# Sixteen instead of eighteen embedding fields by one-hot lookup in a recommender tower, 23 instead of 21 by gather

## What is computed

```
e = stack([tbl_f[ids[:, f]] for f in 0..38], axis=1)      # 2048 x 39 x 64
z = sum over e of (inner_w @ e)**2                        # 2048 x 128
h = concat([z, dense_ctx], axis=1)                        # 2048 x 144
h = relu(h @ W_top1 + b_top1); h = relu(h @ W_top2 + b_top2)
y = h @ W_top3                                            # 2048 x 1
```

## Time and profile before

| | us |
|---|---|
| median of 3 runs (704.07 to 708.3) | 704.64 |
| the profiled execution, whole time | 704.59 |
| its span, first to last instruction | 702.8 |
| mean granted TensorE clock in it | 0.84 of full |

### The profile page before, as it was taken

One profiled execution on the slowest core, in us unless ns is written; L12 is line 12 of the kernel. 1 busy time (PEld: TensorE's weight loads), 2 busy tenths in 40 slices (PEclk: granted clock), 3 DMA queues, 4 the chain that ended last, 5 costly groups with the idle time before them and its releaser, 6 DMA issues.

```text
span 702.8 us, 10016 instructions
## 1 busy us (share of the span) xinstructions
PE 485.0 (69%) x3376; PEld 413.2 (59%) x3376; DVE 442.3 (63%) x708; ACT 226.9 (32%) x310; POOL 353.6 (50%) x343
## 2 busy tenths in 40 slices
PE   0466322767666877779685977777879677987556
PEld 0356322656655756677574856675767666875334
DVE  0988022759686647767676847774778558945542
ACT  2333000323322333334322433324323243445542
POOL 6888775655656554565645545746465365000000
PEclk9987656989898896989988988999798899996756
DMA  8416113667556636655555746754576445645660
GB/s 226 105 51 175 26 25 81 147 146 181 136 131 156 154 83 148 155 128 147 148 135 117 183 102 142 168 139 111 139 166 147 115 123 134 150 107 147 150 165 0
DMA packets 59024, 91.17 MB, mean 130 GB/s; under 512 B 14155, under 2 KB 21064, under 8 KB 58962
## 3 DMA queue, kind: packets, MB, share of 16 engines
q1 hardware_dynamic: 35244, 57.07, 33.1%
q10 hardware_dynamic: 12984, 22.47, 11.6%
q0 software_dynamic: 10752, 11.03, 8.5%
HBM read 27.19 MB, written 0.08 MB: 39 GB/s over the span
## 4 chain that ended last, share of the span: by engine, by line
PE 37%; issue 18%; DVE 16%; DMA 11%; another core or an unknown queue 9%; SPq 4%; ACT 3%; ACTq 1%; DVEq 0%
PE side L400 17%; DMA xs<-xl 8%; DVE onehot L606 6%; PE delta L452 5%; PE turned L441 5%; DVE zp L626 4%; PE side L423 4%; PE side L416 3%; DVE x_all L620 2%; SPq L264 2%; DVE xl L614 2%; ACT sq_all L517 1%; PE side L428 1%; DMA idh<-ids 1%
## 5 line engine op out<-in xcount | busy, mean ns | idle before, releaser
L358 POOL DMA_INDIRECT x_all<-tbl,idx x336 | 352.9, 1050 | 243.8 <-issue 124.9
L400 PE MATMUL side<-table,onehot 125*128 125x192 bf16 x2496 | 275.7, 273 | 119.0 <-issue 69.4
L400 PEld LDWEIGHTS side<-table,onehot 125*128 125x128 bf16 x2496 | 235.2, 109 | 158.5 <-issue 115.6
L517 ACT ACTIVATE sq_all<-delta 128x1024 f32<-128x1024 f32 x128 | 130.8, 1023 | 119.8 <-PE delta L452 54.3
L452 PE MATMUL delta<-xs,ws 117*128 117x512 f32 x240 | 120.8, 532 | 69.3 <-issue 29.0
L626 DVE TENSOR_REDUCE zp<-sq_all 128x128 f32<-128x2048 f32 x64 | 146.1, 2282 | 19.9 <-ACT sq_all L517 15.1
L620 DVE TENSOR_REDUCE x_all<-side 128x128 f32<-128x384 f32 x144 | 78.7, 552 | 114.3 <-remote 72.5
L606 DVE TENSOR_SCALAR onehot<-idh,row_no 125x1024 bf16<-125x1024 f16 (+1 forms) x352 | 137.5, 458 | 17.6 <-DMA idh<-ids 17.6
L503 ACT ACTIVATE xh<-turned 117x512 fp32r<-117x512 f32 x96 | 53.8, 561 | 232.4 <-PE turned L441 93.2
L614 DVE TENSOR_TENSOR xl<-turned,xh 117x512 fp32r<-117x512 f32 x96 | 61.6, 642 | 71.8 <-ACT xh L503 42.7
L452 PEld LDWEIGHTS delta<-xs,ws 117*128 117x128 f32 x240 | 50.7, 224 | 82.7 <-issue 40.2
(11 more groups left out here) (32 smaller groups left out, 93.1 us busy)
## 6 DMA issues: line engine op xcount, KB each, us to landing
xs<-xh ACTq DMA_DIRECT2D x80, 234.0 KB
xs<-xh SPq DMA_DIRECT2D x80, 234.0 KB
xs<-xl SPq DMA_DIRECT2D x80, 234.0 KB
x_all<-tbl,idx POOLq DMA_INDIRECT x336
idh<-ids SPq DMA_DIRECT2D x7, 672.0 KB
idh<-ids SPq DMA_DIRECT2D x7, 336.0 KB
xs<-xh ACTq DMA_DIRECT2D x16, 117.0 KB
xs<-xh SPq DMA_DIRECT2D x16, 117.0 KB
```

The costliest lines, as they stand in the source:

```text
L358: pool.indirect_dma_start(x_slots[k][:, f, 0:E], None, tables[f], bass.IndirectOffsetOnAxis(idx[k][:, f:f + 1], 0),).then_inc(gathered[k], 16)
L400: mm = pe.matmul(side[n % 2][:, q * PARTS * E:(q + 1) * PARTS * E], hot_of[g][:, c, 2 * (k - GROUPS[g][0]) + q, h * TB:(h + 1) * TB], tabl ...
L517: act.activation(to, delta[m % 2][:, :, :, :], ACT.Square).then_inc(squared, 1)
```

## The change

The last pair of fields with 1250-row tables is no longer looked up but gathered. PAIRS falls from 9 to 8, N_ONEHOT from 18 to 16 and GATHERS rises from 21 to 23; the batches of a half become 3, 4, 4, 4, 4, 4. The fifth group of comparisons, the one with a single pair, is gone, and the slots of the others are spread: lookups are due every 1.68 slots instead of 1.5, the comparisons of groups 2 and 3 at slots 5, 6 and 11.5, 12.5 instead of 4, 5 and 9.5, 10.5. `IDS_AT` stays at 6 and 17.5. In the start, one pair's table loads, splits, comparisons and lookups fall away.

```diff
--- before.py
+++ after.py
@@ -24,11 +24,11 @@
 
 KP = 125
 WIDE = (slice(0, 112), slice(112, KP))
-PAIR_CH = [8] * 6 + [10] * 3
+PAIR_CH = [8] * 6 + [10] * 2
 PAIRS = len(PAIR_CH)
 N_ONEHOT = 2 * PAIRS
 PARTS = 3
-GROUPS = [(0, 1), (2, 3), (4, 5), (6, 7), (8,)]
+GROUPS = [(0, 1), (2, 3), (4, 5), (6, 7)]
 NG = len(GROUPS)
 GROUP_OF = {k: g for g, pairs in enumerate(GROUPS) for k in pairs}
 IDS_PARTS = (slice(0, 12), slice(12, N_ONEHOT))
@@ -55,7 +55,7 @@
 
 L = 2 * QUADS
 START = -6.5
-JOBS = [("look", (n // 2, n % 2), -3.9 + 1.5 * n) for n in range(2 * PAIRS)]
+JOBS = [("look", (n // 2, n % 2), -3.9 + 1.68 * n) for n in range(2 * PAIRS)]
 JOBS += [("mlp", part, at) for part, at in enumerate((22.3, 23, 23.8, 24.6))]
 assert len(JOBS) % 2 == 0
 UNIT_AT = [QUADS * h + 3 * u for h in range(2) for u in range(UNITS)]
@@ -68,7 +68,7 @@
 JOB_LAG = 0.4
 FILL_LAG = 0.6
 READ_LAG = -0.2
-HOT_AT = [(-9.5, -8.5), (-0.5, 0.7), (4, 5), (9.5, 10.5), (15.5, 16.5)]
+HOT_AT = [(-9.5, -8.5), (-0.5, 0.7), (5, 6), (11.5, 12.5)]
 IDS_AT = (6, 17.5)
 
 LOOKS = 2 * PAIRS
@@ -111,7 +111,7 @@
         in_sq = sq_all[0:KP, :, :].rearrange("p k c -> p (k c)")
         STAGE = 2 * 10 * E
         homes = [in_x[:, k * STAGE:] for k in range(4)] + [in_sq[:, k * STAGE:] for k in range(3)]
-        home_of = [0, 1, 2, 3, 4, 5, 6, 4, 5]
+        home_of = [0, 1, 2, 3, 4, 5, 6, 4]
         stage = [homes[home_of[k]][:, 0:2 * ch * E].rearrange("p (q c e) -> p q c e", q=2, c=ch)
                  for k, ch in enumerate(PAIR_CH)]
 
@@ -601,7 +601,7 @@
                         if g >= 2:
                             dve.wait_ge(looked, at_looks(s) + 2 * GROUPS[g - 2][-1] + 2)
                         elif not (isinstance(s, int) and s == -1):
-                            dve.wait_ge(looked, at_looks(s - 1) + 2 * GROUPS[4 if g == 0 else 3][-1] + 2)
+                            dve.wait_ge(looked, at_looks(s - 1) + 2 * GROUPS[NG - 2 + g][-1] + 2)
                     for c in range(part * ch // 2, (part + 1) * ch // 2):
                         ins = dve.tensor_scalar(hot_of[g][:, c, :, :], idh[:, 2 * pairs[0]:2 * pairs[-1] + 2, :],
                                                 row_no[ch][:, c:c + 1], None, ALU.is_equal)
@@ -689,7 +689,7 @@
                         dve.tensor_tensor(ws[0:F, :], ws_f[0:F, :], ws[0:F, :].bitcast(F32), ALU.subtract).then_inc(w_low, 1)
                     if k >= 2:
                         fill_first(k - 2)
-                    if k in (1, 3, 5, 7):
+                    if k in (1, 3, 5):
                         for part in range(2):
                             make_hot(-1, (k + 1) // 2, part)
                 fill_first(PAIRS - 1)
```

## The result

The changed kernel is slower. Over 19 executions of each, the median is 715.98 us (707.63 to 728.77) against 705.25 (698.19 to 712.56); the ratio is 1.0233 with a 95% interval of 1.0194 to 1.0271. Some executions of any kernel fall into a slower state of the chip, and ratios leave these out. The difference is 10.7 us by the medians of all runs and 16.4 us (13.7 to 19.1) by the ratio, on 704.6. The forecast was 725 us, 20.5 more. The profiled execution after took 715.96 us with a span of 712.8, 10.0 more than the span before, and the whole times are 11.4 apart: the two traces show about the change of the medians, and less than the ratio.

What follows compares the result with a forecast made beforehand. Gathers issued back to back were taken to hold PE, making batch, transpose report and next batch serial. 704.6 + 32.5 + 7.5 - 19 - 1.5 - 2 + 3 gave 725 us, range 695 to 748.

Steps and rivals of the forecast that it cites:

- The mechanism: In POOL's loop: while gathers issue back to back, PE's work is not finished or reported; gathers and PE's progress are serial.
- The gathers' term: 32 more gathers on POOL at 1.25 us each: +32.5 us in the steps, +7.5 us in the start.
- The savings' term: Lookups off PE and comparisons off DVE: -19 us in the steps, -1.5 us after 597, -2 us in the start.
- the reading by busy shares: POOL, the emptiest engine, takes the added gathers in its slack; PE and DVE set the steps: 675 us, chance 0.14.
- list of signs against the forecast: Steps of 71 to 73 us, unchanged steps, an end changed by over 5 us, or transposes usually reported mid-batch.
- the even balance: Over the whole run, gathers cost 0.47 us each (15 us) against savings of 22.5 us: 700 us, chance 0.12.
- the lower bound from the step with half its gathers: Between second mlp layers, 75.2 us with 42 gathers against 64.3 with 19: at least 0.47 us a gather.
- The intervals of three and four gathers: Batch start to next batch start on POOL, means 5.47 and 7.00 us: the fourth gather costs 1.5 us.
- Free gathers: In the steps, PE and DVE set the pace, POOL's slack takes the gathers, 4.0 to 4.5 us saved each: 675 us, chance 0.14.
- The shorter start: In the start, the 17.82 us wait goes with its lookup and step 0 begins that much earlier: 707 us, chance 0.12.
- SP's term: SP's stack DMAs wait behind the load of ids, its comparisons one slot later: 0.5 us a step, +3 us in all.
- The end: Stretch from 597 us on: remaining lookups save 1.5 us; a change of more than 5 us was not foreseen.

## Why the prediction was right

**The mechanism** was that gathers issued back to back hold PE. Three runs show it: without DMAs 104 us go though POOL is busier, with plain DMAs 86, and with pauses between gathers most of PE's work is reported at once. The changed kernel's start shows PE at one instruction every 1.40 us beside the gathers. In the steps it was too strong to call gathers and PE's progress serial: PE starts as many matmuls beside gathers as without, and only the report is late, by 1.4 us in the median. Nor is it enough that POOL issues without a pause. Earlier in the start of the kernel before, where DVE's work stretches the gathers to 3 us each, PE runs 32 matmuls in 2.81 us and the next lookup follows its fill:

```profile
33.05 2.90 POOL L358 DMA_INDIRECT x_all<-tbl,idx  x1 [0.30 <-issue]
...
35.65 2.81 PE L400 MATMUL side<-table,onehot 125*128 125x192 bf16 x32 [0.39 <-DVE x_all L620]
```

What in the indirect form holds PE is not shown.

**The gathers' term**, +32.5 and +7.5, was measured as +35.8 (30.9 to 40.7) together. **The savings' term**, -19, -1.5 and -2, was measured together with SP's as -16.6 (-20.0 to -13.3); the forecast's sum of these four is -19.5. Both terms were right in total, and so was the sum's sign against the reading by busy shares, which gave 675 us.

**Where it lies** was wrong, and that the total came out in spite of it is partly luck, since the errors go opposite ways. The forecast put 5.5 us in the start and some 2.5 a step in the steps. The profiled pair has 12.3 when POOL resumes, 10.5 at the first mlp layer and nothing after. Steps as long as before and transposes reported in the middle of POOL's run (the first two units) were both on my list of signs against the forecast, the first as the even balance's. Two sizes failed. In the steps I took 1.25 us a gather, the run with gathers alone shows 2.6 us for four, 0.65 each, near the lower bound from the step with half its gathers. That bound is 0.52 and not 0.47, since the step of 64.3 us holds 21 gathers; the 19 I used are those of a later window. The savings there were 3.5 us a step instead of 3.0. Up to the first mlp layer the same run shows 20.6 us for 14 gathers more, 1.5 each. The intervals of three and four gathers, from which I took comfort for 1.25, may have compared slots that hold different other work. The uninterrupted run was also longer than I counted, 80 gathers and not 76: the second unit was reported before POOL stopped.

**The rivals.** Free gathers is refuted by the run with gathers alone. So is the even balance as a sum (+15 for the gathers against +35.8), though in the steps its price is nearer than mine. The shorter start was right in its first half: the wait of 17.82 us is gone, and the first unit is reported 37 us earlier. POOL's run goes on and gets longer, which is what I had set against it. With the lookups removed alone the first mlp layer gains nothing either (250.6 against 249.9). Whether the earlier report is why the change loses less up to there than the halves together (10.5 against 21.4) is open.

**SP's term**, +3, stays unresolved: the delayed transfer is there (3.5 us), moving the load brings no gain, and 3 us are below what that run can tell. **The end** behaved as forecast: 80.7 us from the sixth layer on before (702.8 - 622.1), 80.9 after.

The Trainium skill's page "SBUF — State Buffer", section "Who interferes with whom", by which the PE never waits on anyone, does not carry over to this kernel's indirect gathers: the measurements decide against it, by 104 us between the kernel before and the same without DMAs. The section is about the ports of SBUF, and no run shows whether PE is held there or elsewhere.

## What to carry to other kernels

Before moving work to the emptiest engine, look at what the other engines do while it runs. Compare the recorded end of an instruction with the start of the one that waits for it, inside and outside of its batches. Measure the two halves of an exchange each alone: here +36 and -17 us made the +16. Of 16, 18 and 20 fields looked up, 18 is fastest, and the loss stands in another place on either side: ahead of the first mlp layer with 16, in the last step with lookups with 20. Keep indirect gathers from running back to back for long where PE has work: a later pace alone made the kernel 1.7 to 2.6% faster, and a pause after each gather removed most of the hold but left the time within 1% (a single short instruction instead of four, which should leave POOL below the bound, was not tried).

## What the runs showed of the hardware that I had not expected

Beside back-to-back indirect gathers of 128 rows x 256 bytes (0.94 us each, one every 1.25 us) PE started one weight load or matmul every 1.40 us in the long run of the start, instructions that otherwise take 0.1 to 0.5 us, with the DMA engines 23% busy (87 to 122 us of the changed kernel). In the steps its starts are as dense as ever, and its results come 1.4 to 2.0 us late in the median. A pause of 0.58 us of POOL's own instructions between gathers was enough for most of PE's results to come on time; plain DMAs of the same size from the same queue, 0.575 us each, did not hold it. Results reported late show in no busy share: the rows of transposes looked normal, and the high part that waits for them started up to 28 us after their modelled end in the kernel before.
